# The output projection of an attention from two fp32 products a tile in place of six split ones

## The reference

```
x = layernorm(x + mixer(x))          # gated linear recurrence, 64 states
x = layernorm(x + cross_attention(x, ctx))
x = layernorm(x + experts(x))        # 8 experts, each takes its 256 best tokens

# cross_attention: 16 heads of 16, 64 context rows per sequence
Q, K, V = x @ Wq + bq, ctx @ Wk + bk, ctx @ Wv + bv
scores = Q K^T / 4
out = (softmax(scores) @ V) @ Wo + bo

# experts: router logits = x @ Wr + br, softmax over 8 experts,
# top 256 tokens of each expert, silu up-projection, down-projection, weighted add
```

## Time and profile before

| | before |
|---|---|
| median of three runs | 294.92 us |
| the profiled execution's own time | 294.78 us |
| its span, first to last instruction | 292.6 us |
| PE busy | 237.7 us (81%) |
| DVE busy | 195.2 us (67%) |
| ACT busy | 157.1 us (54%) |
| POOL busy | 147.2 us (50%) |
| mean granted TensorE clock | 0.920 of full speed |

### The profile page before, as it was taken

One profiled execution on the slowest core, in us unless ns is written; L12 is line 12 of the kernel. 1 busy time (PEld: TensorE's weight loads), 2 busy tenths in 40 slices (PEclk: granted clock), 3 DMA queues, 4 the chain that ended last, 5 costly groups with the idle time before them and its releaser, 6 DMA issues.

```text
span 292.6 us, 5417 instructions
## 1 busy us (share of the span) xinstructions
PE 237.7 (81%) x1833; PEld 187.5 (64%) x1833; DVE 195.2 (67%) x587; ACT 157.1 (54%) x323; POOL 147.2 (50%) x213
## 2 busy tenths in 40 slices
PE   8999999899979779969897011257999999999990
PEld 4755557666566556847676011226999999999880
DVE  1744467267776658886889688772665867775594
ACT  3653522544377747546521377612757888874353
POOL 6822995722625231155486999227783355554000
PEclk9999999999999999999997655555999999999998
DMA  6961004009056480936900059924347654533655
GB/s 186 301 131 32 1 10 92 9 13 202 3 116 153 87 189 0 194 77 167 312 10 0 2 166 391 304 61 109 105 90 222 159 108 72 128 38 36 173 206 215
DMA packets 33677, 35.61 MB, mean 122 GB/s; under 512 B 10611, under 2 KB 25971, under 8 KB 33395
## 3 DMA queue, kind: packets, MB, share of 16 engines
q1 hardware_dynamic: 30130, 30.90, 38.6%
q0 software_dynamic: 2784, 4.00, 7.9%
q10 hardware_dynamic: 736, 0.38, 0.4%
HBM read 18.16 MB, written 8.19 MB: 90 GB/s over the span
## 4 chain that ended last, share of the span: by engine, by line
PE 23%; DVE 17%; ACT 6%; issue 5%; DMA 4%; POOL 3%; SPq 1%; DVEq 0%; POOLq 0%; ACTq 0%
PE bank L1257 9%; PE bank L1739 6%; DVE junk L2123 3%; DMA Y<-summed_rows 2%; ACT bank L1174 2%; DVE NMF L1958 1%; PE bank L1524 1%; PE bank L1501 1%; DMA summed_rows<-OUT,idx 1%; PE bank L1695 1%; ACT Y L1013 1%; ACT WUH L1050 1%; POOL rstd L844 1%; DMA XG<-routed_rows,idx 1%; DVE junk_n L2158 1%
## 5 line engine op out<-in xcount | busy, mean ns | idle before, releaser
L916 POOL DMA_INDIRECT summed_rows<-OUT,idx x14 | 26.6, 1900 | 27.9 <-DMA summed_rows<-OUT,idx 21.4
L843 POOL TENSOR_SCALAR var_eps<-mean_var 128x1 f32<-128x1 f32 x32 | 7.2, 226 | 53.9 <-DVE mean_var L1951 53.4
L1257 PE MATMUL bank<-FTH,WUH 128*128 128x256 f32 x94 | 27.5, 292 | 0.1
L1257 PE MATMUL bank<-FTL,WUH 128*128 128x256 f32 x94 | 26.6, 283 | 0.0
L1257 PE MATMUL bank<-FTH,WUL 128*128 128x256 f32 x94 | 26.6, 283 | 0.0
L1174 ACT ACTIVATE bank<-bank,b_up_c 128x256 f32<-128x256 f32 (+1 forms) x48 | 19.5, 446 | 12.9 <-PE bank L1257 12.9
L1958 DVE TENSOR_REDUCE NMF<-bank 128x8 f32<-128x512 f32 x32 | 21.2, 678 | 6.4 <-PE bank L1466 6.3
L1739 PE MATMUL bank<-WDH,MH 128*128 128x256 f32 x80 | 23.2, 290 | 1.3 <-DVE ML L2255 1.3
L906 POOL DMA_INDIRECT XG<-routed_rows,idx x16 | 16.3, 1020 | 14.8 <-DVE idx L2217 10.2
L1739 PE MATMUL bank<-WDH,ML 128*128 128x256 f32 x80 | 22.6, 282 | 0.0
L1739 PE MATMUL bank<-WDL,MH 128*128 128x256 f32 x80 | 22.6, 282 | 0.0
(11 more groups left out here) (367 smaller groups left out, 755.1 us busy)
## 6 DMA issues: line engine op xcount, KB each, us to landing
WDR<-in_L_ffn_W_down SPq DMA_DIRECT2D x8, 640.0 KB
QS<-QH SPq DMA_DIRECT2D x32, 128.0 KB, 2.8
WUR<-in_L_ffn_W_up SPq DMA_DIRECT2D x4, 682.0 KB, 5.2
routed_rows<-X SPq DMA_DIRECT2D x2, 1056.0 KB, 9.9
X<-in_x SPq DMA_DIRECT2D x4, 512.0 KB, 5.0
QS<-QL SPq DMA_DIRECT2D x16, 128.0 KB, 2.5
summed_rows<-X SPq DMA_DIRECT2D x2, 1024.0 KB, 7.4
Y<-summed_rows SPq DMA_DIRECT2D x8, 256.0 KB, 5.5
```

The lines of the kernel that those rows point to most:

```text
L916: pool.indirect_dma_start(summed, bass.IndirectOffsetOnAxis(ap=idx[:, 2 * e + h:2 * e + h + 1].bitcast(U32), axis=0), OUT[:, (2 * e + h) % ...
L1257: last = pe.matmul(o, a, b, start=(n == 0), stop=(n == 3 * len(pairs) - 1))
```

## The change

`ATH`, `ATL`, `WOL` and the copy `wo_s` are gone. Wo is loaded straight into `WO` (fp32, 264 columns a row), and each tile takes two plain fp32 products of `ATT` with `WO`. With that go ScalarE's copies and VectorE's subtractions of them (eight pairs of 128x512, and one pair for the weight in the first stage). `attended(k)` itself now waits until the products of the half block two before have read `ATT`. The z2 products use banks 6 and 1 in turn; the first sums take bank 6 in place of 0, the last val bank 4 in place of 1. The wrw product goes from unit 7 to unit 6, and one ScalarE copy brings it to `WO`. The tables are made from unit 11 on, and none in units 23 and 24.

```diff
-    THROUGH_UNIT = 7
+    THROUGH_UNIT = 6
-    LATE_Z2_BANKS = (6, 4, 5, 6)
-        WO = [place(n, [P, KC, RW], F32R) for n in ("WOH", "WOL")]
+        WO = place("WO", [P, KC, RW], F32)
-        TABLES_AT = {19: (0, 1), 20: (3, 2), 21: (4,), 22: (5, 6), 23: (7, 8), 24: (9,)}
+        TABLES_AT = {11: (0, 1), 12: (3,), 18: (2,), 19: (4,), 20: (5,), 21: (6, 7), 22: (8, 9)}
-                product(("sums", SUMS_AT[g]), 0)
+                product(("sums", SUMS_AT[g]), 0 if SUMS_AT[g] else 6)
-                product(("val", k), 1 if k == HALVES - 1 else 7)
+                product(("val", k), 4 if k == HALVES - 1 else 7)
-                product(("z2", t), 6 if t < NT - TPB else LATE_Z2_BANKS[t - (NT - TPB)])
+                product(("z2", t), 1 if t > 2 and t % 2 else 6)
...
-            pool.wait_ge(w_lo, 3)
+            pool.wait_ge(w_lo, 2)
...
-                for k in SPREAD_AT.get(g, ()):
-                    wait_moved(act, ("spread", k))
-                    if k >= 2:
-                        wait_filled(act, ("z2", 2 * (k - 2) + 1))
-                    act.activation(ATH[:, k % 2], ATT[:, k % 2], ACT.Copy).then_inc(ath_made, 1)
...
-                pe.wait_ge(atl_made, k + 1)
+                wait_moved(pe, ("spread", k))
                 if t == 0:
                     wait_moved(pe, "wrw")
-                split_matmuls(o[:, 0:RW], [
-                    ((ATH[:, k % 2, c, i * P:(i + 1) * P], ATL[:, k % 2, c, i * P:(i + 1) * P]), both(WO, ALLP, c, ALLP))
-                    for c in range(KC)
-                ]).then_inc(sem_filled(("z2", t)), 1)
+                for c in range(KC):
+                    last = pe.matmul(o[:, 0:RW], ATT[:, k % 2, c, i * P:(i + 1) * P], WO[:, c, :],
+                                     start=(c == 0), stop=(c == KC - 1))
+                last.then_inc(sem_filled(("z2", t)), 1)
...
             def attended(k):
                 wait_filled(dve, ("spread", k))
                 wait_moved(dve, ("val", k))
+                if k >= 2:
+                    wait_filled(dve, ("z2", 2 * (k - 2) + 1))
...
-            def attended_low(k):
-                dve.wait_ge(ath_made, k + 1)
-                dve.tensor_tensor(ATL[:, k % 2], ATT[:, k % 2], ATH[:, k % 2].bitcast(F32), ALU.subtract)\
-                    .then_inc(atl_made, 1)
```

More of the change, by code:

```diff
@@ L208, in decoder_block @@
         ATT = place("ATT", [P, 2, KC, HALF], F32)
-        ATH = place("ATH", [P, 2, KC, HALF], F32R)
-        ATL = place("ATL", [P, 2, KC, HALF], F32R)
         PW = place("PW", [NS, L + 1, NS], F32, offset_of["ATT"])
         PB = place("PB", [NS, 6, NS], F32, end_of["PW"])
-        TW = place("TW", [NS, 9, NS], F32, offset_of["ATL"])
-        HS = place("HS", [NS, B, CH + 1], F32, end_of["TW"])
-        assert end_of["HS"] <= end_of["ATL"]
+        TW = place("TW", [NS, 9, NS], F32)
+        HS = place("HS", [NS, B, CH + 1], F32)
         NMF = place("NMF", [P, TPB, HD], F32)
@@ L230, in decoder_block @@
         rcp = place("rcp", [P, NT], F32)
-        wo_s = place("wo_s", [P, KC, D], F32)
         wot_s = place("wot_s", [P, KC, D], F32)
@@ L559, in decoder_block @@
         bo_added = sem("bo_added")
-        spread_made, atl_made = sem("spread_made"), sem("atl_made")
+        spread_made = sem("spread_made")
         low_digit, sel_in, qm_made, qm_in = \
@@ L627, in _ @@
             sp.dma_start(WQ[:], wq.rearrange("(c p) n -> p c n", p=P)).then_inc(wq_in, 16)
-            sp.dma_start(wo_s[:], wo.rearrange("(c p) n -> p c n", p=P)).then_inc(wo_in, 16)
+            sp.dma_start(WO[:, :, 0:D], wo.rearrange("(c p) n -> p c n", p=P)).then_inc(wo_in, 16)
             with nc.allow_non_contiguous_dma(reason="short bias columns"):
@@ L664, in _ @@
                     sp.wait_ge(km_made, 4)
-                    sp.wait_ge(w_lo, 3)
+                    sp.wait_ge(w_lo, 2)
                 for q in range(PR // KC):
@@ L932, in whole @@
                 act.wait_ge(arrived, 16)
-                act.activation(w[0][:, :, 0:src.shape[2]], src[:], ACT.Copy).then_inc(w_hi, 1)
+                act.activation(w[0][:], src[:], ACT.Copy).then_inc(w_hi, 1)
             whole(WIN, win_s, win_in)
@@ L954, in _ @@
                     whole(WG, wg_s, wg_in)
-            whole(WO, wo_s, wo_in)
             def gate_out(g):
@@ L1085, in _ @@
                             act.wait_ge(km_made, 4)
-                            act.wait_ge(w_lo, 3)
+                            act.wait_ge(w_lo, 2)
                         elif n >= 2:
@@ L1124, in _ @@
                     wait_filled(act, "wrw")
-                    act.activation(WO[0][:, :, D:RW], bank_of("wrw")[:, 0:KC * E].rearrange("p (c e) -> p c e", c=KC),
-                                   ACT.Copy).then_inc(through_hi, 1)
+                    act.activation(WO[:, :, D:RW], bank_of("wrw")[:, 0:KC * E].rearrange("p (c e) -> p c e", c=KC),
+                                   ACT.Copy).then_inc(sem_moved("wrw"), 1)
                 if g == LARGEST_UNIT:
@@ L1410, in _ @@
             wait_moved(pe, "w1")
-            pe.wait_ge(w_lo, 3)
+            pe.wait_ge(w_lo, 2)
             pe.wait_ge(wout_in, 16)
@@ L1543, in weight_turned @@
                         at = d * D + c * P
-                        last = pe.transpose(o[:, at:at + P], wo_s[:, c, d * P:(d + 1) * P], ident[:])
+                        last = pe.transpose(o[:, at:at + P], WO[:, c, d * P:(d + 1) * P], ident[:])
                 last.then_inc(sem_filled("wot"), 1)
@@ L1788, in low @@
                 dve.wait_ge(w_hi, n)
-                at = slice(0, src.shape[2])
-                dve.tensor_tensor(w[1][:, :, at], src[:], w[0][:, :, at].bitcast(F32), ALU.subtract).then_inc(w_lo, 1)
+                dve.tensor_tensor(w[1][:], src[:], w[0][:].bitcast(F32), ALU.subtract).then_inc(w_lo, 1)
             low(WIN, win_s, 1)
@@ L2002, in biased @@
                     .then_inc(biased_made, 1)
-            def through_low():
-                dve.wait_ge(through_hi, 1)
-                dve.tensor_tensor(WO[1][:, :, D:RW], bank_of("wrw")[:, 0:KC * E].rearrange("p (c e) -> p c e", c=KC),
-                                  WO[0][:, :, D:RW].bitcast(F32), ALU.subtract).then_inc(sem_moved("wrw"), 1)
             def centred():
@@ L2081, in _ @@
                     attended(k)
-                for k in SPREAD_AT.get(g, ()):
-                    attended_low(k)
                 for c in range(KC):
```

7 lines of the change are left out of this document (1 added, 6 removed).

## The result

The changed kernel took 291.19 us (median of its runs; 294.85 for the kernel before beside it), 3.66 us less. The ratio on record is 0.9858 with a 95% interval of 0.9822 to 0.9894 (the quotient of the two medians is 0.9876): a gain that is clear of the scatter and lies between 1.1 and 1.8%. The forecast was 288.5, its own range 287.0 to 290.0, and the range with the rivals 286.3 to 291.8. The direction held, and so did the wider range; the forecast's own range did not. The gain is 58% of the 6.3 forecast, and the time lies next to rival 1's 291.3, though, as will be seen, not for rival 1's reasons.

A forecast was written before the change was run, and what follows sets the result against it. TensorE bounds two windows of units 13 to 26 and idles 7.02 us in four others; GpSimd bounds the end. Gains 1.0 + .5 + 4.8 = 6.3 us off 294.78 gave 288.5 us, own range 287.0 to 290.0, with rivals 286.3 to 291.8.

The forecast's parts named there:

- rival 1: Other waits replace those removed; ScalarE's exponentials or QS loads hold TensorE in units 13 to 26: 291.3 us, chance .12.
- Rival 2: The plain fp32 product is a third dearer than the split one, .28 us more a tile: 291.7 us, chance .07.
- (a): Units 6 to 8: wrw a unit earlier removes the transposes' 1.58 us wait, less .59 on NMT: gain 1.0 us.
- (b): Units 11 and 12: sums in bank 6 end the 1.54 us wait on REC, tables beside GpSimd's add: gain .5 us.
- (c): Units 13 to 26: no ATH and ATL, a second z2 bank, fewer late tables: gain 4.8 us, window by window.
- the held cast: VectorE's cast NMS of 128 x 16, beside GpSimd's add of bo_all, took .60 us and ended with that add.
- rival 4: Slower: the granted clock's fall moves into units 13 to 24, some 20 to 27 us more: about 310, chance .05.
- The tile's price: On TensorE, a plain fp32 tile of 264 columns takes .89 us against .84 split, .05 more a tile.
- Window 7: The stretch from 157.25, 7.30 us long, set by GpSimd's scales and normalisations: gain 0.
- (d): GpSimd's add of b_out may start up to 10.02 us earlier, one DMA gets another destination: 0, between -.5 and +.5 us.

The follow-up runs named there:

- e7: The changed kernel with the wrw product back in unit 7: 290.37 us, ratio 0.9845.
- e3: The changed kernel with four useless fp32 products of 128x256 put into TensorE's wait just ahead of the first sums in unit 11: 289.50 us, ratio 0.9817.
- f1: The changed kernel with e3's useless products in unit 11 and the tables in units 19 to 24, as in the kernel before: 289.75 us, ratio 0.9808.
- e1: The kernel before with only the two plain fp32 products a tile; banks, wrw and tables as before: 293.20 us, ratio 0.9945.
- f2: The changed kernel with e3's useless products, tables 0, 1, 3 in units 13 and 15, z2 in bank 6 alone (last four 6, 4, 5, 6): 289.61 us.
- f3: The changed kernel with e3's useless products, tables 0, 1, 3 in units 13 and 15, z2 products in reduced fp32 without low parts: 286.69 us.
- g1: The changed kernel with four useless products in unit 8, ahead of the transposes of block 2: 290.81 us, ratio 0.9835.
- e5: The changed kernel with table parts 0 and 1 in unit 13 and part 3 in unit 15, in place of units 11 and 12: 289.10 us.

## Why the prediction held, and where it failed

The wider range held, but in part by luck: it reaches up to 291.8 for the sake of rivals 1 and 2, neither of which came, and what brought the time there was a fall of the clock that the sum has no term for. Of the 6.3 us, (a) was to give 1.0, (b) .5 and (c) 4.8; the cut trace has 3.40.

- **(a)** held: wrw waits for the copy NMT, .63 where .59 was taken, and the transposes wait for nothing; units 6 to 10 are .86 shorter, .66 of it by wrw's place (e7).

```profile
82.36 1.06 PE L1541 MATMUL bank<-wr_s,wot_s 128*128 128x8 f32 x8 [0.63 <-ACT NMT L1083]
```

- **(b)** came out with the other sign: units 10 to 14 are 1.36 longer. The runs make this up from four parts: the clock +1.63 (after less e7), the tables +1.12 (e3 less f1), the sums in bank 6 -1.83 (e7 less e1, without the tables), and .44 that is there in e1 already, .33 of it a longer wait on REC. What turned the sign is the clock. Without the fall, in e7, these units take 18.32, .27 less than before and .71 less than in e1, and the .5 lies between. The bank gave more than the 1.3 taken for it, and the tables cost about what was feared: they were held beside the add, as the held cast had shown. The Trainium skill ("SBUF — State Buffer", "Who interferes with whom"), cited there, puts tensor-scalar operations in their two-port modes among those that lock each other out with GpSimd; `colm_i`, 1.64 us beside the add and .22 without, agrees. That nothing of the gain would come back, which the prediction took from it, did not come true in e7.
- **The clock** was thought of, as rival 4, but as all or nothing and for units 13 to 24, and what spoke against it there was that the change takes gaps away. What came was one short fall in unit 11, ahead of which the change leaves TensorE's gaps as they were. It costs 1.57 on the sums; the useless products win 1.2 of that back (e3).
- **(c)** held within .6 (4.2 for 4.8), with one wrong reason. "the second bank takes the 3.6 of TensorE's waits on X" was wrong: 2.3 of the 3.6 went with the split products (e1), and the .9 that the second bank takes don't shorten the trace (f2). From unit 14 on 3.02 of the 3.90 come with the unsplit products alone (50.43 to 47.41 in e1), and .81 with the tables out of the last units (f1). That TensorE is the bound there is shown by f3. `var_eps` of tile 11 stands at 154.03 in place of 157.33, 3.3 us earlier where 6.3 was looked for; what is missing was lost in unit 11.
- **The tile's price** was undersized a little. Busy time of TensorE in the first five windows is 33.54 against 32.72, .08 a tile for ten tiles, where .05 was taken. It shows in another place than the prediction said: from its start to the next product's the tile takes .70 to .80, and .99 ahead of the sums and the spread products, not .89, but the score product behind it then takes .42 to its successor in place of .24. The same tile before and then after:

```profile
124.74 0.40 PE L1490 MATMUL bank<-QS,KS 128*128 128x512 f32 x1
124.98 0.39 PE L1466 MATMUL bank<-KM,QH 128*128 128x512 f32 x1
```

```profile
124.86 1.06 PE L1522 MATMUL bank<-WO,ATT 128*128 128x264 f32 x4
125.56 0.58 PE L1478 MATMUL bank<-QS,KS 128*128 128x512 f32 x1
125.98 0.39 PE L1454 MATMUL bank<-KM,QH 128*128 128x512 f32 x1
```

- **Rival 2**'s .28 a tile is out. The Trainium skill's four passes ("FP8 and Floating Point Precision", "TensorE Precision Notes") would have made it so; the trace does not agree, as two plain products here cost only .08 more than six reduced ones did.
- **Rival 1** gave the right time for a wrong cause: TensorE's waits on the exponentials at the scores fell (.6 before, .4 after), and no wait on QS loads came up in units 13 to 22.
- **Window 7 and (d)** held: 7.32 us for 7.30, and GpSimd's add of b_out starts at 19.64 in place of 27.47 without showing anywhere later.
- **The range's sum** was off: the best ends of (a), (b) and (c) are 1.58, 1.3 and 6, which gives 285.9, below the 286.3 that was to take them in.

By the cut trace the 3.40 are: the unsplit products 2.79, wrw .66, the place of the tables -.31, the clock -1.57, the second bank 0 or nearly. What is left, 3.40 - 1.57 = 1.83, belongs to the sums in bank 6, which end the wait on REC. No run moves the sums alone, but two others agree: that wait is 1.87 in e1, and e7, which differs from e1 in the sums' bank, the tables' place and the second bank, is 81.59 - 80.02 = 1.57 shorter, 1.88 with the .31 of the tables.

## What to carry to other kernels

Taking work off an engine that feeds the bound pays until the bound is full: here 10.6 us of VectorE time were worth 3.0 from unit 14 on (e1), and that it would be far less than 10.6 could be read beforehand from the idle time of TensorE window by window. Work that is moved to where VectorE has room must be held against what GpSimd does in that moment, and waits that remain unchanged are no proof that the clock does. A bank that is waited for is not always short: ask first what stands ahead of its reader.

## What had not been expected

- Useless products in a wait of 1.09 us made the kernel faster: the sums behind it took 1.77 in place of 3.34 us.
- The same two waits ahead of the same products left the clock at 1.00 in the profiles of four kernels (before, e1, e7, g1) and came with half of it in those of two (the changed kernel, profiled twice, and e5); the fall lasted 3.4 us (99.3 to 102.7).
- A VectorE instruction on 128 x 128 integers takes .22 us alone and 1.64 beside a GpSimd add that had started first, while four of 128 x 1 beside the same add were not held.
- Every execution of the kernels without the split has 1.8 to 2.0 us outside the span (two of f3's have 2.4 and 2.5), every one of the kernel before 2.1 to 2.3; why is open.
